# Group norm of the next image moved into the last steps of the attention

## The reference

```python
def _gn(v, G=32, eps=1e-5):
    g = v.reshape(B_, G, C_ // G, H_, W_)
    ...
    return ((g - m) / jnp.sqrt(s + eps)).reshape(v.shape)
...
x_qubits = x_tokens @ preproj_w.T + preproj_b
x_qubits = x_qubits - x_qubits.mean(axis=1, keepdims=True)
std = jnp.std(x_qubits, axis=1, keepdims=True, ddof=1) + EPS
theta = jnp.pi * jnp.tanh(x_qubits / std)
...
attn = jax.nn.softmax(scores, axis=-1)
v = xh.transpose(0, 2, 1)
out = jnp.einsum('bst,btc->bsc', attn, v)
```

## Time and profile before

| | us |
|---|---|
| median of 3 runs | 8894.9 |
| lowest and highest | 8869.99, 8911.1 |
| profiled execution, its own time | 8893.74 |
| its span | 8891.9 |
| mean granted TensorE clock | 0.927 |

### The profile page before, as it was taken

How to read it: one execution, slowest core, us unless ns; L and a number is a source line. 1 busy time by engine, 2 the same in 40 slices (tenths; PEclk the granted TensorE clock), 3 DMA queues, 4 the chain that set the end, 5 groups by cost and what they waited for, 6 DMA issues and landing times.

```text
span 8891.9 us, 100645 instructions
## 1 busy us (share of the span) xinstructions
PE 7769.1 (87%) x37518; PEld 3840.2 (43%) x37518; DVE 5690.7 (64%) x9661; ACT 3846.1 (43%) x7430; POOL 2243.6 (25%) x1862
## 2 busy tenths in 40 slices
PE   7999999999999975788888888889888988988877
PEld 4555555555555542233443443443443443343343
DVE  5665666666666655466766766766766766776664
ACT  4444455545444442544354354354354344344320
POOL 1222222222222210041241242242142143133152
PEclk9999999999999996889999999998999999999988
DMA  1111111111111111044444454454354454454465
GB/s 64 36 36 36 41 37 46 42 41 41 40 37 36 36 65 39 4 148 126 118 153 126 116 160 124 116 161 129 105 164 134 111 156 141 115 149 155 111 189 137
DMA packets 244230, 850.06 MB, mean 96 GB/s; under 512 B 46412, under 2 KB 49176, under 8 KB 243360
## 3 DMA queue, kind: packets, MB, share of 16 engines
q1 hardware_dynamic: 150272, 388.71, 16.3%
q0 software_dynamic: 92160, 453.06, 16.0%
q10 hardware_dynamic: 1312, 1.87, 0.1%
HBM read 602.10 MB, written 89.68 MB: 78 GB/s over the span
## 4 chain that ended last, share of the span: by engine, by line
PE 39%; DVE 14%; ACT 4%; issue 4%; DMA 3%; POOL 1%; SPq 1%; another core or an unknown queue 0%; ACTq 0%; DVEq 0%; POOLq 0%
PE ps L2229 8%; PE ps L2678 4%; DVE arena L1919 4%; PE ps L2461 4%; PE ps L2218 3%; PE ps L2657 2%; PE ps L2689 2%; PE ps L2151 2%; PE ps L389 2%; PE ps L2345 2%; PE ps L2135 2%; DMA arena<-img,arena 1%; SPq L2712 1%; POOL arena L2494 1%; DMA arena<-arena 1%
## 5 line engine op out<-in xcount | busy, mean ns | idle before, releaser
L2494 POOL DMA_INDIRECT arena<-img,arena x1152 | 1390.4, 1207 | 2767.4 <-DMA img<-arena 1760.3
L2389 DVE SCALAR_TENSOR_TENSOR arena<-arena 128x384 f32<-128x384 f32 x1152 | 748.1, 649 | 591.5 <-DMA arena<-img,arena 535.8
L1919 DVE TENSOR_REDUCE arena<-ps 128x2 f32<-128x1024 f32 x768 | 894.7, 1217 | 341.8 <-PE ps L2194 339.0
L2074 ACT ACTIVATE arena<-ps 128x512 f32<-128x512 f32 x1536 | 829.3, 599 | 492.8 <-PE ps L2218 327.1
L996 POOL TENSOR_TENSOR arena<-arena 128x512 f32<-128x512 f32 x384 | 444.5, 1164 | 1872.0 <-DMA arena<-decay 1871.7
L2229 PE MATMUL ps<-arena 128*64 128x512 f32 x3072 | 896.1, 668 | 0.0
L2678 PE MATMUL ps<-arena 128*64 128x512 f32 x3072 | 788.4, 635 | 73.5 <-ACT arena L2638 38.2
L2461 PEld LDWEIGHTS ps<-arena 128*96 128x96 f32 x4608 | 534.3, 168 | 208.7 <-issue 200.8
L2461 PE MATMUL ps<-arena 128*96 128x128 f32 x4608 | 587.3, 282 | 26.7 <-DVE arena L2378 26.4
L2218 PE MATMUL ps<-arena 32*128 32x512 bf16 x1536 | 404.2, 408 | 187.2 <-issue 133.5
L1131 DVE TENSOR_TENSOR arena<-ps,arena 128x512 f32<-128x512 f32 x384 | 265.5, 691 | 448.0 <-issue 238.6
(11 more groups left out here) (348 smaller groups left out, 12971.7 us busy)
## 6 DMA issues: line engine op xcount, KB each, us to landing
arena<-arena SPq DMA_DIRECT2D x1024, 144.5 KB
arena<-decay SPq DMA_DIRECT2D x384, 256.0 KB, 3.2
img<-arena SPq DMA_DIRECT2D x162, 384.0 KB, 2.6
arena<-img,arena POOLq DMA_INDIRECT x1152
arena<-y SPq DMA_DIRECT2D x16, 768.0 KB, 6.5
arena<-x SPq DMA_DIRECT2D x16, 768.0 KB
out<-arena SPq DMA_DIRECT2D x16, 768.0 KB
arena<-x SPq DMA_DIRECT2D x16, 512.0 KB, 5.0
```

The costliest lines, as they stand in the source:

```text
L1919: dve.tensor_reduce(out, self.wides[B.at("max", b, g, n, h) // 2].rearrange("p (a b) -> p a b", a=2), AX.X, AL.max).then_inc(*S.mark("max_ ...
L2074: act.activation(self.p[n % 6], B("score", b, n)[:, :], ACT.Exp).then_inc(*S.mark("p_act", b, n))
L2389: dve.scalar_tensor_tensor(gb[:, 0:384], gb[:, 384:768], pp[:, 1, n:n + 1], gb[:, 0:384], AL.mult, AL.add).then_inc(*S.mark("corner_x", b, n))
L2494: pool.indirect_dma_start(self.g[n % 6], None, img, bass.IndirectOffsetOnAxis(ap=ii[:, n:n + 1], axis=0)).then_inc(*S.landed(f"{self.tag}g ...
```

## The change

For images 1 to 15 the group norm's steps are emitted in t = 46 to 53 of the attention of the image before; only image 0 keeps them at its head. TensorE's bank for them is then bank 3 and its seven fillers go. In the head the transposes and the projection move from step 7 to step 0, the variance from 8 to 2, `u`'s scaling (L1854) from 9 to 4, the tanh from 10 to 6; the circuits stay in step 11 and behind it, so an image still has 128 steps. The first digits of `PACE` are spread anew with the same sums over steps 0 to 11.

```diff
@@ class GroupNorm @@
-    def pe(self, pe, b):
+    def pe(self, pe, b, i=None):
...
-        ps, free = self.B.hold((self.nm, b), (A, b, "ln"))
+        ps, free = self.B.hold((self.nm, b), (A, b, "ln"), i)
         pe.wait_ge(*free)
-        spin(pe, self.C, ps, {"gn1": 7, "gn2": 0, "gn3": 6}[self.nm])
+        spin(pe, self.C, ps, {"gn1": 0 if b else 7, "gn2": 0, "gn3": 6}[self.nm])
@@ class Layer1, dve @@
-        yield from self.gn.dve(dve, b, x, xg, [("image", b, "sum", 1)])
-        yield from skip(3)
+        if b == 0:
+            yield from self.gn.dve(dve, b, x, xg, [("image", b, "sum", 1)])
+        yield from skip(4 if b else 3)
         dve.wait_ge(*S("u_act", b, "inv"))
         dve.tensor_tensor(u, u, s[:, 0:512], AL.mult).then_inc(*S.mark("u_dve", b))
-        yield
-        yield
+        yield from skip(7 if b else 2)
...
+        gn = self.gn.dve(dve, b + 1, self.xs[(b + 1) % 3], xg, [("image", b + 1, "sum", 1)]) if b + 1 < self.NB else iter(())
         for t in range(54):
             if t == 39:
                 finish(0)
             if t == 44:
                 self.dve_add(dve, b + 1)
+            if t > 45:
+                next(gn, None)
             yield
         finish(1)
@@ act @@
-        yield from self.gn.act(act, b)
-        yield
+        if b == 0:
+            yield from self.gn.act(act, b)
+            yield
...
         act.activation(a, u, ACT.Square).then_inc(*S.mark("u_act", b, "sq"))
-        yield
+        yield from skip(2 if b else 1)
...
         act.activation(a, a, ACT.Exp, scale=-1.0).then_inc(*S.mark("u_act", b, "inv"))
-        yield
-        yield
+        yield from skip(4 if b else 2)
...
         act.activation(u, u, ACT.Tanh).then_inc(*S.mark("u_act", b, "theta"))
-        yield
+        yield from skip(5 if b else 1)
...
+        gn = self.gn.act(act, b + 1) if b + 1 < self.NB else iter(())
...
+            if t > 45:
+                next(gn, None)
             yield
@@ pe @@
-        yield from self.gn.pe(pe, b)
-        yield
+        if b == 0:
+            yield from self.gn.pe(pe, b)
+            yield
...
         i.then_inc(*S.mark("u_pe1", b))
-        yield
+        yield from skip(2 if b else 1)
...
         pe.matmul(ps[:, :], C["B36"], s[:, 0:512], start=True, stop=True).then_inc(*S.mark("u_var", b))
-        yield
-        yield
-        yield
+        yield from skip(9 if b else 3)
...
+        gn = self.gn.pe(pe, b + 1, 3) if b + 1 < self.NB else iter(())
...
+            if t > 45:
+                next(gn, None)
             yield
@@ PACE, the first 16 digits of each string @@
-PACE = ("5400002103093700...
+PACE = ("0304040433303700...
-        "5000001123201010...
+        "0202020222201010...
-        "5000000222300020...
+        "0202020222200020...
```

More of the change, by code:

```diff
@@ L2728 @@
 START = (-70, -40, -39)
-PACE = ("5400002103093700013600007001109209996000400000000007020621002011"
+PACE = ("0304040433303700013600007001109209996000400000000007020621002011"
         "2053100202000000033643000000000000002411100100901000000412000010",
-        "5000001123201010201423061000504220400010401121212314223330012011"
+        "0202020222201010201423061000504220400010401121212314223330012011"
         "1331111003000000033300000000082000200411100101710100000403000002",
-        "5000000222300020101234070200043200320123000222112134223321012011"
+        "0202020222200020101234070200043200320123000222112134223321012011"
         "1502111021000000034270000010000000241330013320500100300501100074")
```

## The result

The changed kernel takes 8989.2 us (median of 4, 8971.15 to 8995.07) against 8901.8 (4 runs): ratio 1.010, 95% interval 1.0075 to 1.0125. It is slower; 8923 was forecast, and 8970 was the end of the range. On the profiled executions the span went from 8891.9 to 8987.3 us, +95.4.

The account below looks back on a forecast made before the run. VectorE's order, then the chain through the inverse deviation, bounds the boundary between images. 14 boundaries at 38.2 instead of 35.5 us (+38) and image 1 (-9) give +29: 8923 us against 8894.9, range 8868 to 8970.

Parts of the forecast that it names:

- the wait ahead of the scaling: VectorE, step 4: the scaling waits 6.6 us for the inverse deviation where it waited 3.1, with ten gather steps behind it.
- the clock ahead of the inverse deviation: TensorE, transposes to variance: taken at full clock, nothing charged; half clock was charged only behind the later pause.
- the supply of gathered tiles: Gathers run six ahead and the pause holds them back: nothing added, up to 1 us at the high end.
- Statistics in VectorE's gap: Statistics, 2.46 us, move to step 120 into VectorE's 4.13 us idle and cost nothing; aggregation ends at 5559.4.
- Mean, variance, normalized image: Attention's tail: TensorE waits from 5558.1 to 5559.4, mean to L434 takes 3.4 us, normalized image out at 5564.3, 11.9 earlier.
- Ten fillers uncovered between u and its variance, and the clock there: TensorE, head: fillers' 4.59 us lose their cover; with one gather step's matmuls the chain is 5.3 us longer, variance ending 5576.9.
- Behind the wait: VectorE after the scaling: ten gather steps, weighing and one more gather step, 11.8 us together, through at 5592.2.
- The pause on TensorE: TensorE waits 7.5 us for the second weighing; 4.7 us of work follow, plus 1.5 us for half clock.
- B: Rival: clock stays down behind each pause, 4.7 us, gathers lag up to 1; boundary near 42 us, 8975; chance 0.22.
- C: Rival, faster: VectorE is never short of work at the boundary, 30.3 us each, 8812 us; chance 0.14.
- D: Rival: the boundary's shift is swallowed later in the image, only image 1's gain is left, 8886 us; chance 0.18.
- Image 1: First image's head, without a gather stream: 12.9 us of finish and group norm become about 4, -9 us (7 to 11).

Follow-up runs that it names:

- E4: Changed kernel plus seven fillers on TensorE where it waits for the normalized image, ahead of the transposes; 1.0029 of the kernel before.
- E2: Changed kernel with only VectorE's scaling of u put back from step 4 to step 9; 1.0021 of the kernel before.
- E8: Changed kernel with the head's steps (transposes, variance, scaling, tanh) back where they were, new PACE digits kept; 1.0026 of the kernel before.
- E10: Changed kernel plus seven fillers ahead of the transposes, ten fillers moved to layer 2's fifth block, scaling in step 6; 1.0008 of the kernel before.
- E3: Changed kernel without the ten fillers between u and its variance; 1.0026 of the kernel before.
- E5: Changed kernel plus 16 fillers where TensorE waits for the second weighing; 1.0109 of the kernel before.
- E12: E6 with two gather steps drawn from step 127 to step 124, ahead of the normalized image; 0.9914 of the kernel before.
- control profiles: Profiles of the kernel before and the changed kernel, both unedited; the changed one's control runs took 1.0117 and 1.0074 of the kernel before.
- E7: Changed kernel with the PACE digits of the kernel before, new head steps kept; 1.0070 of the kernel before.
- E11: E10 with two gather steps drawn from step 127 to step 124, ahead of the normalized image; 0.9976 of the kernel before.
- E1: Kernel before with only the group norm moved into the attention's tail and its fillers gone, old head steps and digits; 0.9959 of the kernel before.
- E6: E1 plus 10 fillers ahead of layer 2's fifth block, where TensorE is idle; 0.9945 of the kernel before.

## Why the prediction was wrong, point by point

The sign and the wait ahead of the scaling were right, the size was not: 14 boundaries of 42.8 us where 38.2 were forecast. Two terms failed, of about equal size: the clock ahead of the inverse deviation, charged at nothing, and the supply of gathered tiles, put at nothing as well. On image 7's clock, with 20.0 taken off:

**Statistics in VectorE's gap.** Right: 5570.04 is ahead of the waits for tiles, and the aggregation ended at 5557.4 in place of 5559.4.

**Mean, variance, normalized image.** Forecast out at 5564.3, measured 5562.8. TensorE did not wait for the aggregation at all (1.3 us forecast), and from the start of the mean to L434 it took 3.2 us (3.4 forecast).

**Ten fillers uncovered between u and its variance, and the clock there.** Right for the fillers: L389's 20 records stand between L2109 and L2116. From the first transpose to the variance's end I took 12.6 us at full clock; it was 15.8 (5582.85 to 5598.62). The stretch 5582.2 to 5592.4 ran at 0.50 of the clock, 1.2 of 2.4 GHz, behind TensorE's 3.16 us without a matmul. That gap was in my own times, since TensorE has nothing between the group norm's last matmul and the normalized image at 5564.3, and I charged half clock only behind the later pause. This is the first term that failed. E4 fills the gap: the inverse deviation comes 4.2 us sooner and the boundary is 38.3 us. (That this is the forecast's number is luck in part: E4's inverse deviation stands 1.8 us ahead of the forecast's, and what is behind it takes 1.9 us more.) From the normalized image to the inverse deviation I took 15.4 us; the mean is 18.3, and 14.1 in E4, so at full clock my sum for it was 1.3 us too long. With the earlier start, the inverse deviation came 1.7 us and the scaling's end 1.8 us later than forecast, and VectorE waited 9.94 us in place of 6.6.

**Behind the wait.** This is the second term that failed. I wrote that gathers run six ahead, that the pause holds them back, and "I add nothing for that and up to 1 us at the high end". From the scaling's end to G50's end I took 11.8 us of work; it was 14.8, of which 2.5 is waits for tiles in G45 and G47 to G50. And the supply is more than an addition to the wait: with the wait at under 0.5 us (E2, E8, E10) the waits for tiles grew to 4.9 to 5.4 us and the boundary stood at 37 to 38 us. In E3 and E4, at about the same length, it is still the chain that sets it.

**The pause on TensorE.** Forecast 7.5 us without a matmul and 1.5 us for half clock behind it; measured 8.44 and, from the weighing's end (5610.20) to L1867, 8.3 us in place of 4.7 + 1.5. The Trainium skill's rule ("TensorE: Matmul & The Clock Gate", Part 1), that a paused TensorE falls to the throttled clock, held here: 0.50 from 5606.1 to 5616.3. The prediction gives 42 us for this rule alone; by its own terms the sum is 38.2 - 1.5 + 4.7 = 41.4. E5 shows that of this end only about 1 us is the clock's alone, since G50's tile comes as late.

The sum for image 7: 1.8 us the chain, 0.5 us a gather ahead of the second weighing, 2.1 us the end, 4.4 in all, 42.6 against the forecast's 38.2. On the mean of the 14 it is 2.4 us up to the inverse deviation (26.2 against 23.8) and 2.2 us behind it (16.6 against 14.4).

**The rivals.** B, the slower one, was nearest (42 us a boundary, 8975), and had 0.22. It named the clock and the gathers, but its number is partly luck: it put 4.7 us of half clock at the end, where E5 finds about 1, and none ahead of the inverse deviation, where E4 finds 4.2. C (30.3 us a boundary) is what the move can reach with VectorE kept in work: E12 has 31.2, but not in this change. D, that the shift is swallowed later and only image 1's gain is left, is refuted: the kernel is slower in all three measurements. The control profiles (+80.9 us in the boundaries, +47.2 in the span) leave open that a part of the shift is swallowed.

**Image 1.** -8.1 us measured, -9 forecast.

What stays open: E7's 1.0070; how much of the supply's limit is the order of blends and how much POOL's long issues, which no run parted; and what E10 would take with its pause filled, since its end ran slowly.

## What to carry to other kernels

When a step is moved ahead in an engine's order, count what stands behind its wait, and then what that releases on the other queues: here the second half of a blend released the gather six numbers on, and the normalized image, the finish and the scaling's wait on VectorE each stopped POOL as well. The first 4 us taken out of the chain came back in full (E3, E4), the next 4 hardly at all (E10), because a buffer's release had nearly the same end; test the two with an edit that makes one better and the other worse, as E11 does. Fillers belong to the wait that they cover: when the order around them changes they are work on the path, and any new gap needs its own.

## What the runs showed of the hardware

Issuing one indirect gather takes POOL between 0.94 and 4.59 us, and the length goes with what VectorE does beside it. In E10, from 4600 to 6600 us, the 59 gathers with no two-input instruction of VectorE (L2400, L2406 and the like) beside them took at most 0.99 us, and all of the 92 above 1.3 us have such instructions beside them. The 170 with them all along took 0.94 to 4.59 us, with a median of 1.08, so a busy VectorE does not always make an issue long. The long ones end at a like place: 0.8 us after a run of VectorE's work ends, in E10 at 5571.71 behind the scaling's end at 5570.89, and so in the timelines of the kernel before, E2, E8 and E11 (3.98 to 3.99 us); in the changed kernel it is 0.5 us (the 1.94 us at 5590.08). No run tried the two engines by themselves, so that one causes the other is read from the rows, not shown.

The chips differ by 3% in this kernel (8628 and 8641 against 8893 and 8900 us). From E1 and E6 that is 17 us for each image (310.4 and 327.3), all of it outside the boundary; a kernel's time on one chip is no reference for another's.
